# The slots of a fused attention and quantized feed-forward kernel written anew with six to seven slots of lag

## The reference

```python
x = x + attention(layernorm(x), rope(ctx))     # scores, softmax over 64 keys, context, output projection
x = x + ffn(layernorm(x))
# attention, per head h (all weight products are folded once ahead of the loop):
scores = q_r @ k_r.T ; attn = softmax(scores) ; ctx_c = attn @ kv_rope ; out = fold(ctx_c)
# ffn = bitlinear158(gelu(bitlinear158(x, w1)), w2), hidden width 1024
def bitlinear158(x, w):
    xn = x / max(norm(x), 1e-12) * sqrt(dim)
    scale = 127 / clip(max(abs(xn)), 1e-5)
    xq = clip(round(xn * scale), -128, 127) / scale      # one scale for each token
    wq = clip(round(w * s), -1, 1) / s                   # s = 1 / clip(mean(abs(w)), 1e-5)
    return xq @ wq.T
```

## Time and profile before

| | us |
|---|---|
| median of 3 runs (lowest, highest) | 455.36 (455.26, 457.75) |
| the profiled execution | 457.08 |
| its span, first to last instruction | 454.9 |
| TensorE, VectorE busy in it | 393.1, 330.5 |
| ScalarE, GpSimd busy in it | 257.8, 255.2 |

### The profile page before, as it was taken

How to read it: one execution, slowest core, us unless ns; L and a number is a source line. 1 busy time by engine, 2 the same in 40 slices (tenths; PEclk the granted TensorE clock), 3 DMA queues, 4 the chain that set the end, 5 groups by cost and what they waited for, 6 DMA issues and landing times.

```text
span 454.9 us, 8971 instructions
## 1 busy us (share of the span) xinstructions
PE 393.1 (86%) x2855; PEld 282.0 (62%) x2870; DVE 330.5 (73%) x873; ACT 257.8 (57%) x477; POOL 255.2 (56%) x321
## 2 busy tenths in 40 slices
PE   9799889794988999989999999999999997876554
PEld 7587557572665776767676767676767674464222
DVE  0364867584798789887878787878787888877564
ACT  1155543332667676675758585858585857556340
POOL 1209447994365656667373738373837373767543
PEclk9899999996999999999999999999999999999665
DMA  8993254443213232424262434252424253443333
GB/s 216 404 333 128 56 142 117 119 117 92 64 52 78 62 79 71 102 48 106 73 107 71 108 73 105 72 107 71 108 72 107 72 107 77 102 127 81 78 97 92
DMA packets 65533, 48.81 MB, mean 107 GB/s; under 512 B 50384, under 2 KB 55888, under 8 KB 65104
## 3 DMA queue, kind: packets, MB, share of 16 engines
q1 hardware_dynamic: 64880, 44.72, 37.8%
q10 hardware_dynamic: 608, 3.54, 2.3%
HBM read 31.98 MB, written 4.46 MB: 80 GB/s over the span
## 4 chain that ended last, share of the span: by engine, by line
POOL 34%; issue 31%; PE 15%; DMA 7%; DVE 6%; SPq 4%; ACT 1%; POOLq 1%; ACTq 0%; DVEq 0%
POOL cl L440 7%; POOL tq L463 6%; POOL qb L466 6%; POOL xa L455 3%; DMA wq_s<-wq 3%; POOL xq L458 3%; POOL yc L450 2%; POOL xn L315 2%; PE hps L786 2%; POOL w_s L478 2%; SPq L365 2%; DMA shift<-nmax 2%; PE ps L744 2%; PE ps L690 2%; DVE cr L953 1%
## 5 line engine op out<-in xcount | busy, mean ns | idle before, releaser
L440 POOL TENSOR_TENSOR cl<-cr,ch 128x512 fp32r<-128x512 f32 x64 | 80.3, 1277 | 131.0 <-ACT ch L550 131.0
L690 PE MATMUL ps<-xh,ah 128*128 128x256 f32 x256 | 75.6, 295 | 4.9 <-ACT g L565 4.5
L754 PE MATMUL hps<-bh,ch 128*128 128x256 f32 x256 | 76.7, 300 | 1.4 <-POOL cl L440 1.4
L534 ACT ACTIVATE qf<-ps 128x512 f32<-128x512 f32 x64 | 37.5, 586 | 65.4 <-PE ps L692 65.4
L755 PE MATMUL hps<-bl,ch 128*128 128x256 f32 x256 | 72.2, 282 | 0.0
L756 PE MATMUL hps<-bh,cl 128*128 128x256 f32 x256 | 72.2, 282 | 0.0
L691 PE MATMUL ps<-xl,ah 128*128 128x256 f32 x256 | 71.9, 281 | 0.0
L692 PE MATMUL ps<-xh,al 128*128 128x256 f32 x256 | 71.8, 280 | 0.0
L550 ACT ACTIVATE ch<-cr 128x512 fp32r<-128x512 f32 x64 | 39.3, 631 | 55.0 <-DVE cr L953 55.0
L690 PEld LDWEIGHTS ps<-xh,ah 128*128 128x128 f32 x256 | 48.2, 188 | 26.7 <-issue 25.8
L786 PE MATMUL hps<-w2q,qt 128*128 128x256 bf16 x256 | 39.1, 303 | 17.3 <-DMA qt<-qb 12.8
(11 more groups left out here) (136 smaller groups left out, 830.2 us busy)
## 6 DMA issues: line engine op xcount, KB each, us to landing
rb<-rinv_d SPq DMA_DIRECT2D x64, 256.0 KB, 3.9
xs<-x SPq DMA_DIRECT2D x8, 512.0 KB, 4.3
out<-yo SPq DMA_DIRECT2D x32, 128.0 KB, 3.5
wq_s<-wq SPq DMA_DIRECT2D x2, 1024.0 KB, 14.4
w_s<-w_t SPq DMA_DIRECT2D x2, 1024.0 KB, 7.2
wo_s<-wo_t ACTq DMA_DIRECT2D x1, 2048.0 KB, 11.1
wk_a<-wk_t SPq DMA_DIRECT2D x2, 512.0 KB, 7.3
kvs<-kvn SPq DMA_DIRECT2D x8, 128.0 KB, 4.1
```

Source lines behind the costliest of these rows:

```text
L440: pool.tensor_tensor(cl[:, u % 2, :, b * S:(b + 1) * S], cr[:, :, b * S:(b + 1) * S], ch[:, u % 2, :, b * S:(b + 1) * S].bitcast(F32), ALU ...
L690: pe.matmul(o, ah[:, c, cols], xh[:, k % 2, c, :], start=(c == 0), stop=False)
L754: pe.matmul(O[:, 0:D], c_h, bh[:, hp, :], start=(hp == 0), stop=False)
```

## The change

The slots are written anew on all five engines, and `LAST` falls from 42 to 38.

- Lags: `project` and `residual` of tile `n-2` come in slot `n` (they were one slot later), `up` of tiles `n-5` and `n-4` together in odd slots, `down` of tiles `n-5` and `n-6` together in even slots, one of them now in the upper half of bank `T`, `finish` at the start of the next odd slot.
- VectorE: in each slot `quadrant_max(n)` comes first (behind `finish` in odd slots), then `divide(n-2)`, and `row_max(n)` and `row_sum(n-1)` stand behind the division (they stood ahead of it).
- TensorE: `contexts(n-1)` follows right behind `turned(n)`, ahead of queries, `shifts(n)` and the projection; it stood behind `shifts(n)`.
- `norms` moves from VectorE (14 instructions) to GpSimd (6, with a power instead of Newton's steps).
- ScalarE loads the Gelu table by a small activation at the end of even slots.
- `x_t(k)` comes a slot earlier (`x_t(2)` in slot 0), and GpSimd makes its tiles before the loop.

```diff
-LAST = NT + 10
+LAST = NT + 6
@@ VectorE's loop
                 for n in range(LAST):
+                    if n % 2 and tile(n - 7):
+                        finish(n - 6)
+                        finish(n - 7)
                     if tile(n):
                         quadrant_max(n, 0)
                         quadrant_max(n, 1)
-                    if tile(n - 4):
-                        x_max(n - 4)
-                    if n % 2 == 0 and 0 <= (n - 6) // 2 < NB + 2:
-                        norms((n - 6) // 2)
+                    if tile(n - 2):
+                        divide(n - 2, 0)
+                        divide(n - 2, 1)
+                    if n % 2 == 0 and tile(n - 4):
+                        x_max(n - 3)
+                        x_scale((n - 4) // 2)
                     if tile(n):
                         row_max(n)
                     if tile(n - 1):
                         row_sum(n - 1)
-                    if tile(n - 2):
-                        divide(n - 2, 0)
-                        divide(n - 2, 1)
...
@@ TensorE's loop
                     if tile(n):
                         scores(n)
...
+                    if n % 2 and tile(n - 5):
+                        up(n - 5, 0)
+                        up(n - 5, 1)
+                    if n % 2 == 0 and k < NB:
                         queries(k, b)
+                    if n % 2 and tile(n - 5):
+                        up(n - 4, 0)
                     if n <= NT:
                         turned(n)
+                    if n % 2 and tile(n - 5):
+                        up(n - 4, 1)
+                    if tile(n - 1):
+                        contexts(n - 1)
+                    if n % 2 and k < NB:
+                        queries(k, b)
+                    if n % 2 == 0 and n // 2 + 2 < NB:
+                        x_t(pe, n // 2 + 2)
                     if k < NB:
                         queries(k, b + 1)
...
+                    if n % 2 == 0 and tile(n - 2):
+                        project(n - 2, 0)
                     if tile(n):
                         shifts(n)
+                    if n % 2 and tile(n - 2):
+                        project(n - 2, 0)
+                    if tile(n - 2):
+                        project(n - 2, 1)
                     if turns(n):
                         kv_t((n + 2) // 4)
+                    if n % 2 == 0 and tile(n - 6):
+                        down(n - 5)
+                        down(n - 6)
@@ GpSimd, the new norms
+                    for h, floor in halves:
+                        pool.tensor_scalar(v[:, 2 * h:2 * h + 2], stat[:, j, 2 * h:2 * h + 2], floor, 1.0, ALU.max, ALU.mult).then_inc(done, 1)
+                    pool.tensor_tensor(r[:, c], v[:, c], mhalf[:, c], ALU.pow).then_inc(done, 1)
+                    pool.tensor_tensor(t[:, c], r[:, c], amax[:, j, c], ALU.mult).then_inc(done, 1)
+                    for h, floor in halves:
+                        pool.tensor_scalar(scl[:, j, 2 * h:2 * h + 2], t[:, 2 * h:2 * h + 2], EPS_Q, wfactor[:, h:h + 1], ALU.max, ALU.mult).then_inc(done, 1)
@@ SyncE's loop
-                for n in range(LAST + 1):
-                    if n % 2 == 0 and tile(n - 6):
-                        turn_x(n - 6)
-                        turn_x(n - 5)
-                    if n % 2 and tile(n - 10):
-                        turn_g(n - 10)
+                for n in range(LAST):
+                    if n % 2 == 0 and tile(n - 5):
+                        turn_g(n - 5)
+                    if n % 2 and tile(n - 7):
+                        store(n - 6)
+                        store(n - 7)
                     if tile(n):
                         shift_rows(n)
...
                     if tile(n - 1):
                         rinv_rows(n - 1)
                         rinv_spread(n - 1)
+                    if n % 2 == 0 and tile(n - 4):
+                        turn_x(n - 4)
+                        turn_x(n - 3)
+                    if n % 2 and tile(n - 5):
+                        turn_g(n - 5)
```

285 lines of the change are left out of this document (133 added, 152 removed).

## The result

The kernel after takes **493.04 us** (median of 4 runs, 490.80 to 496.40) against 455.95 for the kernel before beside it (455.26 to 457.75): ratio 1.081, 95% interval 1.074 to 1.088. The forecast was 474 with a range of 459 to 486: the sign was right, the size was not, and the time lies 7 us above the range. The profiled execution of after took 490.8, the shortest of the four, with a span of 488.9, which is 34.0 more than before, where 18.7 was forecast. Some executions have a lower mean clock and a longer time than the others of the same kernel (three of the four of e_xscale, which therefore has no ratio, and the profiled ones of e_row_early, e_comb_ctx and e_best1).

What follows compares the result with a forecast made beforehand. TensorE's own work was taken to set the pace in slots 7 to 29, waits the other stages. Start +17, middle +12.5, end −10.8 sum to +18.7, making the median 455.4 into 474.1, said as 474; range 459 to 486.

Steps and rivals of the forecast that it cites:

- The failed step: Middle, slots 7 to 29: chains other than the division's wait were said to have room and were costed at nothing.
- The waits of the middle that it did have: Slots 7 to 29: TensorE waiting for the division, the first gelu and residual, 2.2 us a pair; middle +12.5.
- The start: Slots 0 to 6: x_t(2)'s wait in slot 0 and the loop through the reciprocals lengthen it by 17 us.
- One sign that the prediction named against itself: Slots 3 to 6: the prediction is wrong if the division finds its read of the reciprocals already landed.
- each slot lasts at least a turn: Start: each slot lasts at least the loop row_sum, reciprocals' write and read, division, row_max: 1.25 + 0.3 + 10.67 or 11.62 us.
- its upper bound, +20: Start, slots 0 to 6: +20 us if the clock falls in the waits of 3 to 5 us in slots 3 to 6.
- Rival (a): Start: the early loop through the reciprocals doesn't bind, so +7 instead of +17, time 464; chance 0.15.
- (b): Middle: division reaches TensorE before it stands still, so the middle gains 13; time 449; chance 0.07.
- (d): Whole kernel: nothing moves, the shorter end pays for the rest; 452, or 455 to 459; chance 0.07.
- (c): Middle and start: TensorE's clock also falls behind waits, +7 and +3, time 484; chance 0.13.
- The end: Slot 30 to the last instruction: 68.3 us instead of 79.1, so −10.8; bounds −16 and −6.
- The 3.2 us for the read: Start: by the skill page the reciprocals' 512 KB read takes 3.2 us, not 3.9; start +10, time 467.

Runs made afterwards that it cites:

- e_xscale: Kernel after with x_max and x_scale behind row_max and row_sum on VectorE in even slots: 478.76 us.
- e_row_early: Kernel after with row_max and row_sum ahead of the division on VectorE in slots 0 to 7 only: 492.12 us, ratio 1.077.
- e_comb_ctx: e_comb with contexts behind both query blocks in even slots below 30, and ScalarE's copy of the first query block ahead of ctx_hi: 460.72 us, ratio 1.008.
- e_best1: e_comb plus e_scalar1's x_scale, first query block ahead of turned (slots 1, 3), half a ternary_2 step moved to slot 4, slot 4's read before transposes: 458.63 us.
- e_turn: Kernel after with the first transpose of rounded x issued between the reciprocals' write and read on SyncE in even slots: 475.33 us, ratio 1.045.
- e_comb: Kernel after with e_turn's and e_xscale's orders, loads behind the transposes, and norm_x(4), norm_x(5) ahead of rope(1): 461.77 us, ratio 1.010.
- e_scalar1: Kernel after with x_scale's first instruction as two one-column tensor_scalar, constant in the instruction, g_scale's likewise a tensor_scalar: 483.17 us, ratio 1.060.
- e_load: Kernel after with load of x and swap of kv behind the reciprocals' write and read on SyncE, slots 1 to 6: 489.80 us, ratio 1.070.

## Why the prediction was wrong, and where it was right

**The failed step** is the sentence on the middle "The other chains of a slot have room, and so I cost them at nothing". It lists `row_max` to shift, division to `ctx_lo`, and the reciprocals, and not the chain from rounded x over its two transposes to `up`, which the new order puts behind the write and read of the reciprocals and wants at the head of the next slot. TensorE stood 17.2 us for it in slots 7 to 29, and slots 7, 11 and 25 of these lost some 1.6 us each to a low clock as well. Two orders that shorten this chain, e_turn and e_xscale, take 11.1 and 14.1 us off the middle; together, in e_comb, they leave 4.0 us of that wait.

**Its input was off too.** `row_max` was to end 4.6 us into an even slot; it ended at 5.5, since `x_scale` was taken without what it costs beside `ctx_lo` (1.08 us). e_scalar1 removes just that, for 12.6 us in the middle; e_xscale moves it behind, for 14.1. The three repairs overlap, as each alone restores most of the room: the cause is that the chain was 1 to 2 us too long, not one instruction.

**The waits of the middle that it did have** were too large: contexts 0.94 against 1.2 in even slots; 0.44 ahead of the third half of `up` in odd ones, against 0.6 and another 0.3 at the contexts that didn't come. They sum to 1.4 a pair instead of 2.1, so xqt's 1.5 a pair shows as +0.85 on the pair (24.8 against 23.95). That is outside the bound the prediction set for itself (24.6). Part of the missed term was hidden by this, which was luck: without it a pair would have been well under 23.95, as in e_comb, where it is 23.2. e_turn's 274.1 is near the prediction's 276.3 for the middle only because 8.7 us of waits for `xqt` stand in it for waits that were priced too high.

**The start**, forecast +17, measured +20.2 and 1.1 ahead of slot 0. `x_t(2)` waits 2.33 (2.6), and the divisions of tiles 0 to 4 start at 64.17, 76.55, 89.56, 105.71 and 121.84 (64.1, 76.3, 89.5, 104.5, 118.6). The first three agree to 0.3, closer than the same slots agree from one execution to the next, so some of that is luck. The fourth is 1.2 late because 2.8 us lie between the division and `row_max` in slot 4, where the prediction had 1.8; 1.46 of them are `x_max` waiting for GpSimd's centre. The fifth is 3.2 late, since in slot 5 `up` waits 5.4 us for `xqt`, `turned` stands behind `up` and `row_sum(4)` behind `turned`, and its own turn took 12.4 us instead of 11.6. One sign that the prediction named against itself came: in slot 3 the division began at 76.55, 2.4 us into the slot, with no idle time of VectorE before it, so the loop did not set slot 3. What the prediction had too simple is "each slot lasts at least a turn". e_load made the first five turns 0.4 to 2.3 us shorter, 7.0 together, and won 3.3 us; e_row_early cut the loop and won nothing. My reading, which no run shows by itself, is that the loop, SyncE's order, GpSimd's weight work and VectorE's place of the division end close behind each other. The clock fell as well: 0.89 in slot 2 and 0.77, 0.80 and 0.89 in slots 4 to 6, over the start 0.89 where it was 0.96 before. The prediction had that as its upper bound, +20; no run tells its price from that of the waits.

**Rival (a)** can be judged by e_load, which makes its condition true (the read is issued 3.3 us after `row_sum` in most slots): the start then is +17, not +7. Its price was wrong. **(b)** and **(d)** fell with the division at 2.4 to 3.7 us of the slot, as the prediction argued. **(c)**, the clock: slot 11, behind the longest wait of the middle (2.35 us), has a granted clock of 0.88 and lasts 14.6 us, slots 7 and 25 alike, each about 1.6 us longer than its wait explains; slots with waits of up to 1.2 are at 1.00. That is about 5 us in the middle, where (c) had 7, but behind waits for `xqt` that the prediction didn't have, and not behind the contexts' wait.

**The end**, −10.8 forecast, −8.8 measured: 70.3 us against 68.3. It took 70.3 to 73 over all the kernels here, so the sum was 2 to 5 us short, with a clock of 0.76 to 0.83 over the whole of it. The estimate for `norms` on GpSimd, 2.3 us, for which it names no row, came out at 2.6 in slot 20, and nothing waited for it there.

**The 3.2 us for the read**: the Trainium skill (DMA: Bandwidth & Descriptors, section Anatomy of one DMA) would have made the start +10. Issue to landing was 4.1 us (3.9 before), and the first divisions came when the trace's number said: the measurement decides.
